# Attention stage with its first projections reordered, and each batch's weighing two slots closer to its scores

## The reference

```python
q = _rope(_proj(Wq, bq, layernorm(x)), 8)      # per head, half of the channels rotated
k = _rope(_proj(Wk, bk, ctx), 8)
v = _proj(Wv, bv, ctx)
p_attn = softmax(q @ k^T / sqrt(16))
x = x + tanh(g_xattn) * _proj(Wo, bo, p_attn @ v)
gate, up = split(layernorm(x) @ w_gu^T)
y = (silu(gate) * up) @ w_down^T
x = x + tanh(g_ffn) * y / rms(y)
```

## Time and profile before

| | before |
|---|---|
| median of the runs | 728.29 us |
| profiled execution, its own time | 727.19 us |
| its span on the core | 725.4 us |
| PE busy | 689.1 us (95%) |
| DVE busy | 611.1 us (84%) |
| ACT busy | 521.4 us (72%) |
| POOL busy | 476.5 us (66%) |
| first weighing product | at 48.36 us |
| ten steps from 119.8 to 361.3 us | 241.5 us |

### The profile page before, as it was taken

How to read it: one execution, slowest core, us unless ns; L and a number is a source line. 1 busy time by engine, 2 the same in 40 slices (tenths; PEclk the granted TensorE clock), 3 DMA queues, 4 the chain that set the end, 5 groups by cost and what they waited for, 6 DMA issues and landing times.

```text
span 725.4 us, 13353 instructions
## 1 busy us (share of the span) xinstructions
PE 689.1 (95%) x4660; PEld 334.3 (46%) x4660; DVE 611.1 (84%) x825; ACT 521.4 (72%) x925; POOL 476.5 (66%) x403
## 2 busy tenths in 40 slices
PE   3579999999999999999999999999999999999995
PEld 1234434443444344434443444656565556555653
DVE  6599989888988898888889779766899789977894
ACT  2028888888888888888888876665666566666653
POOL 2946555786678667866633129876697669766773
PEclk9559999999999999999999999999999999999999
DMA  6877777787777877877663202000001000100011
GB/s 206 219 184 168 180 197 190 175 184 205 201 173 178 216 184 182 201 197 190 166 150 70 85 24 74 1 1 0 1 1 44 15 1 0 45 16 0 4 42 72
DMA packets 48935, 80.59 MB, mean 111 GB/s; under 512 B 14436, under 2 KB 17892, under 8 KB 48868
## 3 DMA queue, kind: packets, MB, share of 16 engines
q1 hardware_dynamic: 47568, 78.73, 42.6%
q10 hardware_dynamic: 1300, 1.01, 0.5%
HBM read 45.11 MB, written 32.24 MB: 107 GB/s over the span
## 4 chain that ended last, share of the span: by engine, by line
PE 52%; POOL 26%; issue 14%; DVE 4%; DMA 2%; ACT 1%; SPq 0%; POOLq 0%; ACTq 0%; DVEq 0%
PE pv_ps L845 20%; POOL probs L300 15%; PE s_ps L815 14%; PE st_ps L827 9%; POOL probs L304 9%; DVE max_rows L1113 2%; PE st_ps L800 2%; PE st_ps L857 2%; PE st_ps L788 2%; PE st_ps L794 2%; POOL over_stack L224 1%; DMA xt_all<-x_dram 1%; DMA image<-split_rest 1%; DMA qk_stack<-image 1%; ACT probs L950 0%
## 5 line engine op out<-in xcount | busy, mean ns | idle before, releaser
L1113 DVE TENSOR_REDUCE max_rows<-s_ps 128x2 f32<-128x1024 f32 x256 | 305.2, 1212 | 44.9 <-PE s_ps L815 44.1
L950 ACT ACTIVATE probs<-st_ps 128x512 f32<-128x512 f32 x512 | 277.6, 596 | 63.8 <-PE st_ps L827 53.0
L319 ACT ACTIVATE probs<-s_ps,gu_sc 128x512 f32<-128x512 f32 x176 | 117.7, 685 | 84.4 <-PE s_ps L405 84.2
L300 POOL TENSOR_TENSOR probs<-probs 128x512 f32<-128x512 f32 x88 | 120.3, 1371 | 69.4 <-ACT probs L319 69.0
L845 PE MATMUL pv_ps<-probs,v_all 128*32 128x256 f32 x2048 | 163.2, 391 | 2.2 <-ACT pv_all L956 2.2
L815 PE MATMUL s_ps<-qk_stack 48*128 48x512 f32 x512 | 133.7, 519 | 8.4 <-DVE max_rows L1113 7.4
L171 DVE SCALAR_TENSOR_TENSOR proj<-s_ps,gu_sc,proj 128x512 f32<-128x512 f32 x132 | 98.7, 748 | 11.1 <-PE s_ps L405 1.9
L827 PE MATMUL st_ps<-qk_stack 50*128 50x512 f32 x512 | 108.0, 411 | 0.0
L421 PE MATMUL st_ps<-dn_head,over_input 128*128 128x512 f32 x264 | 104.9, 423 | 1.0 <-DVE over_input L182 1.0
L815 PEld LDWEIGHTS s_ps<-qk_stack 48*128 48x128 f32 x512 | 49.7, 191 | 115.8 <-issue 71.7
L845 PEld LDWEIGHTS pv_ps<-probs,v_all 128*32 128x32 f32 x2048 | 40.6, 108 | 97.8 <-ACT probs L950 81.3
(11 more groups left out here) (120 smaller groups left out, 883.6 us busy)
## 6 DMA issues: line engine op xcount, KB each, us to landing
qk_stack<-image SPq DMA_DIRECT2D x60, 384.0 KB, 6.2
image<-split_head SPq DMA_DIRECT2D x31, 256.0 KB
image<-split_head SPq DMA_DIRECT2D x62, 128.0 KB
image<-split_rest SPq DMA_DIRECT2D x31, 256.0 KB
xt_all<-x_dram SPq DMA_DIRECT2D x16, 256.0 KB, 4.0
ct<-ctx_dram SPq DMA_DIRECT2D x16, 256.0 KB, 3.4
scale_of<-inverse_scratch SPq DMA_DIRECT2D x16, 256.0 KB
out_dram<-over_stack SPq DMA_DIRECT2D x16, 256.0 KB, 2.0
```

What stands on the lines that cost most here:

```text
L300: nc.gpsimd.tensor_tensor(pair[:, n], parts[T_ % 2][:, 2 * n], parts[T_ % 2][:, 2 * n + 1], ALU.add).then_inc(pairs_ok, 1)
L319: nc.scalar.activation(parts[T_ % 2][:, k], gu_ps[(2 * k) % BANKS], ACT.Copy, scale=gu_sc[:, k, T_ % IT:T_ % IT + 1]).then_inc(gate_read, 1)
L950: nc.scalar.activation(probs[at % PROBS][:, tile % 4, :], st_ps[item % ST_BANKS][:], ACT.Exp).then_inc(st_read, 1)
L1113: nc.vector.tensor_reduce(out, s_ps[item % S_BANKS][:], AXIS_X, ALU.max).then_inc(s_read, 1)
```

## The change

The first stage is reordered, and `SHIFT = 2` lets a slot do the score that was due two slots earlier.

- PE begins with nine products of 128 by 128 on a tile of ones (`WARM`); they go into `pv_ps`, whose contents nobody uses then.
- The projection of batch 2 stands ahead of `project_v(0)`, and `project_v(0)` and the two small products for biases and gates stand among the first scores.
- 14 scores of batch 0 instead of 16 are done ahead of step 0. In step b, slots 0 and 1 do the scores 14 and 15 of batch b, and slots 2 to 15 the scores 0 to 13 of batch b + 1.
- DVE rotates batch 0 ahead of the statistics and the norm of batch 1, and does the statistics of batch 3 and the two scale conversions ahead of the maxima.
- Of the four stores of batch 0's second half, ACT issues three right after its second projection's bias, and SP the fourth.

```diff
+                store_rest(sp, 0, 1)                      # SP, after store_projection(sp, 0, 0)
...
                 for slot in range(SLOTS):
-                    if b + 1 < B:
-                        score(pe, b + 1, slot)
-                        if slot == V_AT:
-                            project_v(pe, b + 1)
+                    ahead, scored = divmod(slot + SLOTS - SHIFT, SLOTS)
+                    if b + ahead < B:
+                        score(pe, b + ahead, scored)
+                    if b + 1 < B and slot == V_AT:
+                        project_v(pe, b + 1)
                     weigh(pe, b, slot)
...
+                pe.wait_ge(values_set, 1)
+                for _ in range(WARM):
+                    nc.tensor.matmul(pv_ps[:, 0:P], ones[:, 0:P], ones[:, 0:P], start=True, stop=True)
                 pe.wait_ge(weights_in, WEIGHTS)
                 project_rot(pe, 0)
                 project_pass(pe, 0)
-                project_rot(pe, 1)
-                project_pass(pe, 1)
-                pe.wait_ge(wv_in, 16)
-                project_v(pe, 0)
-                project_rot(pe, 2)
-                project_pass(pe, 2)
+                for n in (1, 2):
+                    project_rot(pe, n)
+                    project_pass(pe, n)
...
-                for slot in range(SLOTS):
+                for slot in range(SLOTS - SHIFT):
                     score(pe, 0, slot)
+                    if slot == 3:
+                        pe.wait_ge(wv_in, 16)
+                        project_v(pe, 0)
...
-                    if n == 2:                            # ACT
-                        take_v(act, 0)
-                        store_projection(act, 0, 1)
+                    if n == 1:
+                        store_head(act, 0, 1)
...
-                statistics(dve, 1)                        # DVE
-                normalise(dve, nc.vector, 1)
                 dve.wait_ge(table_in, TABLES)
                 rotate_first(dve)
-                statistics(dve, 2)
-                normalise(dve, nc.vector, 2)
+                for n in (1, 2):
+                    statistics(dve, n)
+                    normalise(dve, nc.vector, n)
+                statistics(dve, 3)
```

More of the change, by code:

```diff
@@ L54 @@
 GROUPS = B // GROUP
-FIRST_TURN, TAIL_AT = 12, 3
+FIRST_TURN, TAIL_AT, WARM = 12, 3, 9
+SHIFT = 2
 BANKS = 4
@@ L76, in transposed_items @@
     for n in range(AHEAD_PROJ):
-        if n == 2:
-            items.append(("v", 0))
         items += [("rot", n), ("pass", n)]
+    items.append(("v", 0))
     for b in range(B):
@@ L906, in _ @@
             def _(pe):
+                pe.wait_ge(values_set, 1)
+                ones = v_ones[0].rearrange("p k j q c -> p (k j q c)")
+                for _ in range(WARM):
+                    nc.tensor.matmul(pv_ps[:, 0:P], ones[:, 0:P], ones[:, 0:P], start=True, stop=True)
                 pe.wait_ge(weights_in, WEIGHTS)
@@ L909, in _ @@
                 project_pass(pe, 0)
-                project_rot(pe, 1)
-                project_pass(pe, 1)
-                pe.wait_ge(wv_in, 16)
-                project_v(pe, 0)
-                project_rot(pe, 2)
-                project_pass(pe, 2)
[L916 to L920, removed]
-                for slot in range(SLOTS):
-                    score(pe, 0, slot)
+                for n in (1, 2):
+                    project_rot(pe, n)
+                    project_pass(pe, n)
+                for slot in range(SLOTS - SHIFT):
+                    score(pe, 0, slot)
+                    if slot == 3:
+                        pe.wait_ge(wv_in, 16)
+                        project_v(pe, 0)
+                    if slot == 5:
+                        pe.wait_ge(wo_in, 16 * 4)
+                        nc.tensor.matmul(pv_ps[:, 0:1], wo[:], bias_v[:], start=True, stop=True).then_inc(spread, 1)
+                    if slot == 6:
+                        pe.wait_ge(gates_in, 32)
+                        pe.wait_ge(consts, 5)
+                        nc.tensor.matmul(pv_ps[:, 2:4], ones_row[:], gate_in[:], start=True, stop=True).then_inc(spread, 1)
                 for b in range(B):
@@ L1014, in _ @@
                         act.dma_start(gu_sc16[:], d["gate_up_scales"]).then_inc(scales_in, 16)
+                take_v(act, 0)
                 act.wait_ge(spread, 2)
@@ L1182, in _ @@
                 nc.vector.memset(ones_row[:], 1.0).then_inc(consts, 1)
-                statistics(dve, 1)
-                normalise(dve, nc.vector, 1)
                 dve.wait_ge(table_in, TABLES)
                 rotate_first(dve)
-                statistics(dve, 2)
-                normalise(dve, nc.vector, 2)
+                for n in (1, 2):
+                    statistics(dve, n)
+                    normalise(dve, nc.vector, n)
+                statistics(dve, 3)
+                dve.wait_ge(scales_in, 16)
+                nc.vector.tensor_scalar(keep["gu_sc"][:, :, 0:IT], gu_sc16[:, :, 0:IT], 4.0 / X_GAIN, None, ALU.mult).then_inc(scales_ok, 1)
+                nc.vector.tensor_scalar(keep["gu_sc"][:, :, IT:GU], gu_sc16[:, :, IT:GU], 16.0 / X_GAIN, None, ALU.mult).then_inc(scales_ok, 1)
                 for slot in range(SLOTS):
                     maxima(dve, 0, slot)
-                    if slot == 1:
-                        statistics(dve, 3)
                     if slot == 7:
@@ L1197, in _ @@
                                                ALU.mult).then_inc(consts, 1)
-                dve.wait_ge(scales_in, 16)
-                nc.vector.tensor_scalar(keep["gu_sc"][:, :, 0:IT], gu_sc16[:, :, 0:IT], 4.0 / X_GAIN, None, ALU.mult).then_inc(scales_ok, 1)
-                nc.vector.tensor_scalar(keep["gu_sc"][:, :, IT:GU], gu_sc16[:, :, IT:GU], 16.0 / X_GAIN, None, ALU.mult).then_inc(scales_ok, 1)
                 for b in range(B - 1):
```

## The result

The changed kernel takes 744.43 us (median of six runs, 737.14 to 752.88) against 728.4 us for the kernel before on the same chip (726.43 to 728.99): 1.020 of its time, 95% interval 1.017 to 1.023. The forecast was 731.8 us within 724.5 to 738. The direction was right, the size was not. The runs of the changed kernel also lie much further apart than those of the kernel before, which the last sections come back to.

A forecast was written before the change was run, and what follows sets the result against it. PE bounds the steps; in the start it waits for transfers and DVE. 727.19 - 4.5 (start) + 0.2 (end) + 7.8 (steps) = 730.7 us as profiled; the median, 1.1 us above, gives 731.8 us, range 724.5 to 738.

The forecast's parts named there:

- What bounds the kernel: Steps: PE is busy all 24.15 us of a step, so every PE wait put into a step is paid in full.
- The mechanism of the steps: Steps: maxima, loaded behind `load_half`, come too late for weighings 2.48 us closer; 0.6 us a step, 7.8 us in all.
- The rival in which the small loads land about 3 us after their issue: Steps: maxima land in time in nearly all steps, leaving the start's gain; 724.0 us, chance 0.27.
- Both chains start at the same score, so a step pays the larger of the two.: Steps: of the lacks at slots 0 and 8, only the larger is paid, 0 to 1.7 us a step.
- The size of the lack: Steps 1 to 13: 0.6 us a step taken, 7.8 us in all, between 0 and 17.
- The start: Before the steps: earlier rotation, stores, statistics and fewer scores, limited by SP and POOL; 4.5 us gained.
- The queue of SP: Start: `load_half(1, 0)` issued at 37.4 us, landing at 44.1 with the maxima behind it; limits the start's gain to 4.3 us.
- The end: Last step: two slots of scores move into it, costing 0.2 us.
- The norm of batch 1: Start: behind the rotation with POOL idle, it takes 0.55 us instead of 2.55 us.

The follow-up runs named there:

- both relieved: Changed kernel (`SHIFT = 2`) with the second transfer of each `load_half` cut to 2 of 48 rows from batch 2 on, in both halves: 726.26 us, ratio 0.998.
- the stage alone: Changed kernel with `SHIFT = 0`: the new first stage, scores 16 slots ahead as before; 724.93 us, ratio 0.997.
- the shift alone: Kernel before with only the `SHIFT = 2` loops put in, its old first stage kept: 751.84 us, ratio 1.025.
- the first half relieved: Changed kernel with the second transfer of `load_half(n, 0)` alone cut to 2 of 48 rows from batch 2 on: 746.46 us, ratio 1.018.

## Why the prediction was right and wrong, point by point

- **What bounds the kernel** was right: no PE wait that was put into a step was won back. The steps' 18.4 us, step 0's 1.2 and the start's 2.7 are all of the difference.
- **The mechanism of the steps** was right, and shown: with fewer bytes in `load_half` alone the time falls to 726.3 us, with the maxima ahead of it their wait is gone. The rival in which the small loads land about 3 us after their issue is excluded, in SP's queue and in ACT's: behind `load_half` they took 3.8 to 6.7 us.
- **The step that failed** is "Both chains start at the same score, so a step pays the larger of the two." They do not. The chain to slot 8 ends its scores with score 15, which stands in slot 1, behind the wait at slot 0; the chain to slot 0 ends its scores with score 7, in slot 9, behind the wait at slot 8. Each is put off by the other's wait, so each pays its own lack. In step 8 of the changed kernel slot 8 costs 1.05 us and the next slot 0 costs 0.74 us. Over 14 steps it is 9.7 + 8.0 = 17.7 us over the kernel with both relieved; the larger of the two in each step would have made 12.4 us.
- **The size of the lack** was the other half of the miss in the steps. I took 0.6 us for the larger lack of a step; it measured 12.4 / 14 = 0.89 us. That 0.6 is near what each single half cost, 0.69 and 0.57 us, is luck: it was not worked out for a half. I also took 13 steps, where the waits stand in 14 steps, and the bound of 17 us does not belong to 1.7 us a step, which makes 22. The working took the 6.2 us of the earlier trace rows for the second transfer of `load_half`, which it mixes with the faster first one. The true room stood in the trace before: from the landing of the maxima to their weighing there were as little as 0.8 us. Against the shift of 2.48 us the rooms of steps 1 to 14 lack 10.6 us if the larger lack of a step counts, and 13.3 us if both do. The rest up to 17.7 us goes with later landings: before, the maxima of the two halves were there 7.3 and 7.7 us after `load_half`'s issue, after it 7.6 and 7.8 us (medians). A wait follows the late ones, and what is early in another step isn't carried over.
- **The start**, 4.5 us forecast and 2.7 us found, was mis-sized in its last link. The rotation came at 8.49 us (8.2 forecast), POOL on batch 1 at 22.09 (21.8). The queue of SP was the link that held, as forecast, but 1.5 us later (the maxima at 45.6 us instead of 44.1):

```profile
8.49 0.69 DVE L1104 TENSOR_TENSOR cross<-proj,sin 128x512 f32<-128x512 f32 x1 [2.10 <-DMA sin<-sin_dram]
...
22.09 2.35 POOL L1046 TENSOR_TENSOR cross<-proj,sin 128x1024 f32<-128x1024 f32 x1 [2.71 <-issue]
...
33.44 2.35 POOL L1046 TENSOR_TENSOR cross<-proj,sin 128x1024 f32<-128x1024 f32 x1
...
38.46 0.79 SPq L613 DMA_DIRECT2D qk_stack<-image  x2
39.30 0.58 SPq L633 DMA_DIRECT2D qk_stack<-max_scratch  x2
```

  POOL ended batch 1 at 33.4 us as worked out (33.2), `load_half(1, 0)` went out at 38.46 instead of 37.4 us, because the last store of batch 1 was issued at 34.01 us and took 4.4 us, and the maxima were there 7.2 us later instead of 6.7, so the first weighing was at 45.67 us. With `SHIFT = 0` and its two more slots of scores it was at 45.96 us. The two slots that the shift takes out ahead of the first weighing, 2.3 us in my sum, bought 0.3 us at most: in the three kernels with cut transfers and `SHIFT = 2`, whose start is the same, the first weighing came at 45.26 to 45.99 us. My sum had nothing for step 0. It took 25.36 us after, 24.21 before and 24.61 in the stage alone, so 0.4 of its 1.15 us come with the stage.
- **The end** (+0.2 us) was 0.0 us.
- **The norm of batch 1** was right: 0.55 us without POOL beside it. The rotation of batch 0 started in this execution on the load of `sin`, landed at 8.46 us, some 0.1 us behind the bias; in the stage alone `sin` was there at 7.88 us and the rotation started on the bias, at 8.49 us too.

My sum with the measured terms: 727.19 - 2.7 + 1.2 + 18.4 = 744.1 us, the profiled execution's 744.07. The forecast for it was 730.7: of the 13.4 us between, 5.3 us are the two lacks counted as one, 4.6 us the size of the larger, 0.7 us what the steps took beyond these lacks, and 2.8 us the start, step 0 and the end. The best kernel of all runs is the first stage without the shift: 724.9 us, ratio 0.997.

## What to carry to other kernels

When work is moved closer to what it feeds, count the room of every chain that crosses the gap and pay each lack separately: a wait moves the start of the next chain along, so lacks within one period add up instead of hiding behind the largest. Take the room against the late landings, not against the median, and look at what a median is taken over: here it was over two transfers, and only the slower one counted. And in these kernels a small transfer issued 2 to 3 us behind a large one landed with it, from SP's queue and no sooner from ACT's; ask what is in flight and not only what stands in the queue.

## What the runs showed of the hardware that was not expected

- A load of 16 KB from ACT's queue, with 768 KB from SP's under way, was there 5.5 us after its issue. A small store behind `load_half` took 6.5 us. With nothing big ahead, the same loads took 1.8 to 2.9 us.
- Kernels whose PE waits often in the steps have runs that lie far apart (737 to 753 us, 740 to 768, 739 to 755), while the new stage alone, with or without warm-up, with one slot of shift, and both kernels with both halves cut stay within 2.2 us. The kernel before, which has none of these waits, is not free of it: of its 65 executions in these measurements one took 739.33 us, at a mean granted clock of 0.923. In three traces, the shift alone, the first half relieved and the load from ACT's queue, the granted clock falls to 0.50 within the steps (in those of the kernels with another order in SP's queue too), as in the 14 us above, or as here with the shift alone:

```profile
186.60:207.10 20.50, 20.50 (x114) 7.65 (x112) 12.51 (x16) 10.61 (x20) 10.67 (x12) 0.50 0.58 145
```

  The three traces have seven such falls. Each began 0.6 to 1.8 us after PE had waited 1.31 to 1.97 us for the maxima. In the 14 us ahead of a fall PE had no other idle stretch above 0.6 us. A wait of 1.35 us ran without a fall, so what sets one off stays open. The profiled execution of the changed kernel, whose longest wait in the steps was 1.2 us, stayed at full clock in its steps, so its 744.1 us are waits alone. Its two slowest executions, 750.07 and 752.88 us, had a mean granted clock of 0.965 and 0.953 against 0.972; they left no trace, so that falls made them slow is argued and not shown.
